# Norms applied by ScalarE, bulk transfers issued at other places in the batch loop, and the routing steps of the last batch in another order

## The reference

```python
mod = (silu(c) @ wmod).reshape(8, 6, 1, 256)            # sa, ca, ga, sb, cb, gb; ga, gb kept away from 0
h = layernorm(x) * (1 + ca) + sa
x = x + ga * attention(h)                               # 32 heads of 8, window of 8 to each side, then proj
h = layernorm(x) * (1 + cb) + sb
x = x + gb * moe(h)                                     # shared MLP (width 352) + top 2 of 16 experts (width 176)
```

## Time and profile before

| | |
|---|---|
| three runs | 449.8, 444.47 and 447.63 us; median 447.63 us |
| the profiled execution | 445.15 us, its span 443.3 us |
| busy share | PE 88%, DVE 61%, POOL 28%, ACT 27% |
| mean granted TensorE clock | 0.935 of full speed |
| batch loop | about 24 to 220 us |
| expert tiles | about 275 to 401 us |

### The profile page before, as it was taken

One profiled execution on the slowest core, in us unless ns is written; L12 is line 12 of the kernel. 1 busy time (PEld: TensorE's weight loads), 2 busy tenths in 40 slices (PEclk: granted clock), 3 DMA queues, 4 the chain that ended last, 5 costly groups with the idle time before them and its releaser, 6 DMA issues.

```text
span 443.3 us, 11573 instructions
## 1 busy us (share of the span) xinstructions
PE 388.4 (88%) x4740; PEld 285.9 (65%) x4740; DVE 269.0 (61%) x515; ACT 120.5 (27%) x261; POOL 124.1 (28%) x131
## 2 busy tenths in 40 slices
PE   7889799795999999966869595999999999999963
PEld 4568588674878888855434374677777777764452
DVE  2678699674899999998864964222222222211566
ACT  1132032220323223201232440233333334331520
POOL 6201031030303030201576670043343343341000
PEclk9999899796999999999968976899999999999968
DMA  8164819978181817160122422133333332103823
GB/s 293 47 137 143 207 50 188 311 168 195 50 205 51 204 50 181 49 176 7 38 103 98 162 90 81 47 109 96 104 106 95 104 105 59 49 2 91 289 72 119
DMA packets 53066, 52.44 MB, mean 118 GB/s; under 512 B 22148, under 2 KB 48045, under 8 KB 52406
## 3 DMA queue, kind: packets, MB, share of 16 engines
q1 hardware_dynamic: 40784, 28.68, 25.0%
q0 software_dynamic: 4528, 12.40, 9.1%
q10 hardware_dynamic: 7702, 10.62, 6.9%
HBM read 28.75 MB, written 20.79 MB: 112 GB/s over the span
## 4 chain that ended last, share of the span: by engine, by line
PE 67%; DVE 15%; issue 11%; DMA 2%; POOL 2%; ACT 1%; ACTq 0%; SPq 0%; DVEq 0%; POOLq 0%
PE bank L1371 14%; PE bank L1386 9%; PE bank L1261 7%; PE bank L1215 5%; PE bank L1150 5%; PE bank L1188 5%; PE bank L1324 4%; PE bank L1197 3%; PE bank L1168 3%; PE bank L1355 2%; PE bank L1379 2%; DMA first_region<-wmod 2%; DVE region L741 2%; PE bank L1230 2%; PE bank L1208 2%
## 5 line engine op out<-in xcount | busy, mean ns | idle before, releaser
L502 POOL DMA_INDIRECT yrows<-second_region,sloti x47 | 46.2, 984 | 91.5 <-ACT second_region L644 91.2
L1023 DVE COPY second_region<-bank 128x256 f32<-128x256 f32 x47 | 20.0, 425 | 84.8 <-PE bank L1355 84.8
L1371 PE MATMUL bank<-region,second_region 128*128 x188 | 66.5, 479 | 0.2 <-DVE second_region L1023 0.2
L1386 PE MATMUL bank<-w,second_region 88*128 x188 | 48.5, 380 | 0.6 <-ACT second_region L639 0.6
L1261 PE MATMUL bank<-xT_region,sw 128*128 128x512 f32 (+1 forms) x96 | 45.2, 626 | 0.0
L449 POOL TENSOR_TENSOR rstd2s<-ve,cft 128x2 f32<-128x2 f32 x8 | 5.7, 708 | 135.8 <-DVE ve L788 135.7
L1371 PEld LDWEIGHTS bank<-region,second_region 128*128 128x128 f32 x188 | 33.1, 196 | 13.5 <-issue 3.9
L1188 PE MATMUL bank<-region,second_region 64*32 64x128 f32 x1024 | 33.1, 276 | 8.2 <-issue 8.2
L467 POOL DMA_INDIRECT hslots<-hx,posi x32 | 35.5, 1110 | 16.3 <-issue 9.0
L1188 PEld LDWEIGHTS bank<-region,second_region 64*32 64x32 f32 x1024 | 28.0, 109 | 16.0 <-issue 16.0
L1324 PE MATMUL bank<-sw,second_region 128*128 128x256 f32 (+1 forms) x96 | 27.3, 446 | 10.2 <-DVE second_region L986 5.9
(11 more groups left out here) (159 smaller groups left out, 594.5 us busy)
## 6 DMA issues: line engine op xcount, KB each, us to landing
second_region<-hslots SPq DMA_DIRECT2D x47, 128.0 KB, 2.0
hslots<-zeros ACTq DMA_DIRECT2D x5, 1024.0 KB, 6.3
region<-vd SPq DMA_DIRECT2D x32, 128.0 KB, 5.3
region<-yrows SPq DMA_DIRECT2D x16, 256.0 KB, 6.0
modb<-moddram SPq DMA_DIRECT2D x8, 384.0 KB, 4.7
w<-w2T POOLq DMA_DIRECT2D x4, 704.0 KB, 9.3
xs<-x SPq DMA_DIRECT2D x8, 256.0 KB, 6.7
vd<-second_region SPq DMA_DIRECT2D x8, 256.0 KB, 2.2
```

The costliest lines, as they stand in the source:

```text
L502: gp.indirect_dma_start(yrows, bass.IndirectOffsetOnAxis(ap=sloti[:, s:s + 1], axis=0), yo[:, s % RING, :], None, bounds_check=TOPK * T - ...
L1023: dve.tensor_copy(rT[:, s % 2].rearrange("p c t -> p (c t)"), RTP).then_inc(rT_s, 1)
L1371: last = pe.matmul(UP(s), rT[:, s % 2, c, :], w13[:, c, bass.ds(experts[s], 1), :], start=c == 0, stop=c == C - 1)
L1386: last = pe.matmul(YP(s), hT2[0:IH, s % 2, k, :], w2[:, k, bass.ds(experts[s], 1), :], start=k == 0, stop=k == 1)
```

## The change

Four things are changed together. Line numbers of the new kernel differ from the old one's.

1. Both norms are applied by ScalarE as `x * rstd + off` with `off = -mean * rstd`, but for the first norm of batch 0. VectorE adds the negated mean (`less1`, `less2`), GpSimd a product of two columns (`off1`, `off2`). `ln1_apply(1)` stands on ScalarE between `scaled_h(0)` and `keep_q(0)`; in the loop both stand behind `keep_v`; `ln2_apply(7)` stands ahead of `silu_g(0)`.
2. The zeroing of `hslots` is issued in four parts (11 or 12 tiles of 128 KB each) in iterations 0, 4, 5 and 6, right behind `keep_q`. The first part of the experts' weights follows the first `exponent` of iteration 1.
3. `load_shared` and `load_second` wait for `keep_q(it+1)`. `load_x(b+3)` stands ahead of `modulation(b+1)` and `values_in(b+1)`.
4. In the last batch `count(0)` stands behind `turn_p(7, 0)`, `ranked(0)` and `new_tiles(0)` behind `over_sum(7, 0)`, and `placed(0)` behind `over_sum(7, 1)`.

```diff
-ZEROED = 6
+ZEROED = (0, 4, 5, 6)
@@ sync, batch loop
                     values_out(b + 1)
+                if b + 3 < B:
+                    load_x(b + 3)
+                if b + 1 < B:
                     modulation(b + 1)
                     values_in(b + 1)
-                if b + 3 < B:
-                    load_x(b + 3)
@@ gpsimd
             def rstd1(b):
                 wait(gp, ln_ve, b + 1)
-                gp.tensor_tensor(rstd[:, :], ve[:, :], nhalf, ALU.pow).then_inc(ln_rs, 1)
+                wait(gp, ln_xn, b)
+                pw = gp.tensor_tensor(rstd[:, :], ve[:, :], nhalf, ALU.pow)
...
+                pw.then_inc(ln_pw, 1)
+                gp.wait_ge(ln_pw, b)
+                gp.tensor_tensor(off1[:, :], less1[:, :], rstd[:, :], ALU.mult).then_inc(ln_rs, 1)
...
             def main(it, first, after):
+                if it in (1, 2, 3):
+
+                    gp.wait_ge(q_s, it + 2)
                 if it == 1:
                     load_shared()
@@ scalar
+            def ln1_apply(b):
+                wait(act, ln_rs, b + 1)
+                wait(act, hT_p, b)
+                for u in range(U):
+                    last = act.activation(xn[:, u], xs[:, U * b + u, :], ACT.Identity,
+                                          scale=rstd[:, u:u + 1], bias=off1[:, u:u + 1])
+                last.then_inc(ln_xn, 1)
...
+            def zero(k):
+                if k == 0:
+                    act.wait_ge(pads, 7)
+                a, z = k * NS // len(ZEROED), (k + 1) * NS // len(ZEROED)
+                act.dma_start(hslots_t[:, a:z], zeros[:, :].unsqueeze(1).to_broadcast([P, z - a, D])).then_inc(row_z, 16)
+
             def main(it, first, after):
                 if after:
                     scaled_h(it + 1)
                     keep_q(it + 1)
+                if it in ZEROED:
+                    zero(ZEROED.index(it))
                 exponent(it, 0)
+                if it == 1:
+                    act.wait_ge(mod_p, 3)
+                    act.dma_start(staged[:, :], w13T[:, 0:STAGE]).then_inc(ld_ew, 16)
...
                     keep_v(it + 1)
                 if not first:
+                    ln2_apply(it - 1)
+                if after > 1:
+                    ln1_apply(it + 2)
+                if not first:
                     turned_h(it - 1)
...
             scaled_h(0)
+            ln1_apply(1)
             keep_q(0)
...
+            ln2_apply(B - 1)
             silu_g(0)
@@ vector
+                dve.tensor_scalar(less1[:, :], mv[:, :, 0], -1.0, None, ALU.mult)
...
             def main(it, first, after):
-                if after == 0:
-                    ranked(0)
...
-                elif after == 0:
-                    new_tiles(0)
                 over_sum(it, 0)
+                if after == 0:
+                    ranked(0)
+                    new_tiles(0)
...
-                if not first:
-                    ln2_apply(it - 1)
                 residual(it, 0)
-                if after > 1:
-                    ln1_apply(it + 2)
-                elif after == 1:
+                if after == 1:
                     pick(1, 0)
                     chosen(0)
-                else:
+                over_sum(it, 1)
+                if after == 0:
                     placed(0)
-                over_sum(it, 1)
@@ tensor
                 if after:
                     turn_x(it + 1)
-                else:
-                    count(0)
                 scores(it, 1)
                 if after:
                     make_q(it + 1)
                 turn_p(it, 0)
+                if not after:
+                    count(0)
```

More of the change, by code:

```diff
@@ L713, in _ @@
             ln1_stats(0)
-            ln1_apply(0)
+            dve.wait_ge(ln_rs, 1)
+            for u in range(U):
+                last = dve.tensor_scalar(xn[:, u], xs[:, u, :], mv[:, u, 0:1], rstd[:, u:u + 1], ALU.subtract, ALU.mult)
+            last.then_inc(ln_xn, 1)
             dve.wait_ge(modT_p, 1)
@@ L734, in _ @@
             ln1_stats(1)
-            ln1_apply(1)
             def by_window(it, u):
@@ L787, in ln2_stats @@
                 wait(dve, l2_mv, it + 1)
+                dve.tensor_scalar(less2[:, :], mv2[:, :, 0], -1.0, None, ALU.mult)
                 dve.tensor_scalar(ve2[:, :], mv2[:, :, 1], EPS, None, ALU.add).then_inc(l2_ve, 1)
[L790 to L796 removed]
             links = [0]
```

49 lines of the change are left out of this document (23 added, 26 removed).

## The result

| | before | after |
|---|---|---|
| median of 12 runs each, side by side | 445.18 us (440.1 to 451.8) | 447.09 us (443.3 to 451.6) |
| ratio | | 1.0081, 95% interval 1.0041 to 1.0121 |
| the profiled execution | 445.15 us, span 443.3 | 445.70 us, span 443.9 |
| busy: PE, DVE, ACT, POOL | 88, 61, 27, 28% | 87, 57, 31, 29% |

Executions over 1.5% slower than the fastest of their kernel are left out of this ratio and of every later one (7 of 12 for "transfers only"), and both profiles of the kernel before, that of "norms only" and that of the old order are of such executions.

What follows compares the result with a forecast made beforehand. TensorE, busy 88%, was taken as the bound, with 17.6 us of loop excess at stake. Terms 4.0 + 0.3 - 0.3 - 4.5 + 0.4 = -0.1 us against 445.15; forecast set at 446.0 us, own range 441 to 450, with rivals 434.5 to 454.

Steps and rivals of the forecast that it cites:

- 1, setup: Ahead of the loop: `ln1_apply(1)` delays `keep_q(0)` to 22.5 us, +4.0 us uncovered, plus 0.3 for the clock.
- 2, norms: In the loop: VectorE loses two norm applications per batch, TensorE wins only its waits for VectorE, -0.3 us.
- 3, transfers: In the loop: moved bulk transfers leave 13.1 us of excess instead of 17.6, -4.5 us.
- 4, last batch: End of the loop: `over_sum(7, 0)` ends 3.1 us earlier, but `turn_h(7)` comes +0.4 us (bounds -0.5 and +1.2).
- forecast excess of 13.1 us: Batch loop's time over its floors after the change: 0.9 + 5.5 + 5.0 + 1.7 us, instead of 17.6.
- Iterations 2 and 3: Behind `keep_q`, `w2T` makes a block 3.9 us late or in time; half taken, 0.6 for clock: 2.5 us each.
- rival 1: Placement works: refill slips in ahead of the bulk in iterations 1, 2 and 3, excess 3 to 7 us; chance 0.30.
- Iteration 0: Shared weights' packets leave; a block waits for `values_out`, `load_x(3)` and `modb`, and 0.9 us of excess remain.
- floor of 20.04 us: Iteration 0's least period: TensorE's 21.4 us less 1.36, since `turn_h` and `gate` are missing there.
- Iteration 1: Experts' and shared weights hold a block, gap in `times_v(1, 0)` or `make_v(2)`: 4.2 plus 1.3 for clock, 5.5 us.
- Iterations 4 and 5: Iterations 4 to 6: a zeroing part drains 1 us ahead of the next wanted block, so nothing is lost.
- rival 2: Iteration 1 takes it back: its block behind a 2.7 MB burst is served last, excess 22 us, 454 us; chance 0.20.

Runs made afterwards that it cites:

- transfers only: Kernel before with only the bulk transfers moved to the change's new places (parts 2 and 3 of its list); ratio to the kernel before 1.0014.
- norms only: Kernel before with only the norms on ScalarE, the first norm of batch 1 behind `keep_v(0)`; ratio to the kernel before 0.9926.
- old order: Changed kernel with `count`, `ranked`, `new_tiles` and `placed` of the last batch in the order of before; ratio to the kernel before 1.0092.
- old transfers: Changed kernel with all bulk transfers and `load_x` issued where the kernel before issues them; ratio to the kernel before 1.0139.
- norms and order: Kernel before with the norms on ScalarE (batch 1's first norm behind `keep_v(0)`) and the last batch in the changed order; ratio to the kernel before 1.0030.
- `w2T` in pieces: Changed kernel with only GpSimd's bulk (shared and second weights, 4.0 MB) cut into 11 pieces over iterations 0 to 5; ratio to the kernel before 1.0046.
- setup repaired: Changed kernel with the first norm of batch 1 applied behind `keep_v(0)` instead of ahead of `keep_q(0)`; ratio to the kernel before 1.0040.
- spread version: Changed kernel with batch 1's first norm behind `keep_v(0)` and the 11.4 MB of bulk cut into 39 pieces; 432.88 us, ratio to the kernel before 0.9825.
- bulk late: Changed kernel with every bulk transfer (11.4 MB) issued only in iteration 7; one execution, only its loop to be read, 129.94 us.

## Why the prediction was wrong, point by point

No single pair of these runs parts the four terms cleanly. A weighted fit of four additive parts to the eight comparisons (the change, three versions with a part undone, two parts alone and two pairs) gives them, times 442 us and with 95% bounds:

| part | forecast | fitted |
|---|---|---|
| 1, setup | +4.3 us | +3.7 +/- 1.7 |
| 2, norms | -0.3 | -1.7 +/- 1.7 |
| 3, transfers | -4.5 | +0.6 +/- 1.4 |
| 4, last batch | +0.4 | +2.4 +/- 1.7 |

The fitted sum is +5.1, the change alone measured +3.6 (1.8 to 5.4). That the parts add is assumed; the change lies 1.7 standard errors below the fit, the norms alone 1.4 below it, the version with the old order 1.4 above and that with the old transfers (1.0139) 1.1 above, for which I have no cause. With any one comparison left out, the transfers' part stays between -0.3 and +1.1 us. The others move more: the setup's between +2.5 and +5.4, the norms' between -3.1 and +0.1, the order's between +1.2 and +4.1. So the firm results are that the transfers gained nothing near 4.5 us and that the setup costs.

The last two rows of the forecast are also not cut as the fit cuts them: the +0.4 holds what the norms do at the end, which the fit counts with the norms. Together they compare well: forecast +0.1, fitted +0.7 +/- 1.3, and norms and order alone measured +1.3 (-0.4 to +3.0).

**Part 3 is the step that failed.** It was put at -4.5 us; the fit has +0.6, and the transfers alone have 1.0014, which leaves the forecast outside; only the step from the change to its version with the old transfers (-2.6 +/- 3.6 for the new places) would still allow it. The forecast excess of 13.1 us came out as 16.2 in the trace. The mechanism stood: blocks late behind bursts, shown by the kernel without them. The sizes did not:
- *Iterations 2 and 3*, "in time if it slips in ahead of the bulk. I take the half": it did not slip in. q0's first packet came 1.3 us behind the start of its issue in both iterations (84.5 to 85.8 and 112.0 to 113.3 us), where the kernel before has 2.7 and rival 1 counted on 3.4; by the count of 127 that is over 1 us ahead of the requests, at 87.1 and some 115 us. 27.54 and 24.68 us are 6.1 and 3.3 over the floor, where 2.5 each and a part of the 1.7 were forecast. The two gaps of iteration 2 make 3.85 us of the 6.1, and the granted clock is 0.81 from 92 to 110 us. `w2T` in pieces takes the two iterations to 21.22 and 22.37 us, so it is this burst.
- *Iteration 0*: the block gap of 0.9 us was forecast well (0.77), but my floor of 20.04 us was not one. PE waits 1.50 us for VectorE's residual (L816) there in ten of the sixteen traces; in the other six a block comes 2.1 us or more late just ahead of it and hides part or all of this wait. The period without bulk is 22.12 us. Of the 4.7 us of excess that I put at stake, only 2.6 could be won.
- *Iteration 1*: 25.41 us, 4.0 over the floor instead of 5.5, with the gap in `turn_p(1, 1)` (L1227, 66.47 us), between the two places named, and its packet at 64.0 to 64.5 us, ahead of the 66 to 69 that were forecast with the setup's 4 us.
- *Iterations 4 and 5*: as forecast, within 0.8 us. Iteration 4, with its zeroing part, takes 22.18 us against 21.37 before.

The four traces with the new places (the change, setup repaired, old tail, transfers only) have loops of 143.3 to 146.3 us, the six with the old ones 143.6 to 149.1. So rival 1 (placement works) fell, and rival 2 too: the bursts hold other blocks for about as long. A place that is quiet for `spread_q` isn't quiet for the instruction stream, whose packets come every 3.6 to 7.4 us in the spread version (61 to 121 us).

**Part 1** was right in mechanism and place. `keep_q(0)` came at 21.98 instead of 22.5, because GpSimd's product of two columns takes 0.20 us (0.27 the first time), not 0.5. The first scores came 3.5 us later. The clock's share, 0.3, is a matter of the execution: from `keep_q(0)` to `keep_q(1)` two of seven traces with the delay take 13.97 and 13.99 us, five 12.36, with 12.31 before. The fit has +3.7 for it, the repair alone gives 0.4% (1.0081 to 1.0040), with intervals that overlap.

**Part 2** is open in size. -0.3 lies within the fit's bounds (-3.4 to 0.0), but not within those of the norms alone (0.9926 is -3.3, from -5.5 to -1.0). In the traces quiet periods fall from 21.37 to 21.40 us to 21.22 to 21.24, some 0.16 per iteration; in seven iterations that would be 1.1 us, an estimate, against the 0.3 forecast for a few of them. "TensorE can win only its waits for VectorE" does not hold once the bursts are cut into pieces, where the kernel with the norms on ScalarE has the loop shorter by 4.2 us. ScalarE's new place holds nothing: its periods without bulk are at the floor.

**Part 4** held by the trace, and in part by luck. Against `keep_q(7)` `turn_h(7)` came 1.9 us later, but 1.7 of it lies ahead of `turn_h(6)` (39.13 us behind `keep_q(7)` against 37.47), a stretch that takes 37.5 and 40.5 us in the two profiles of the kernel before, so it shows nothing. From `turn_h(6)` to `turn_h(7)` it is +0.2, where +0.4 was forecast, and the steps are those of the prediction: `placed(0)` starts 0.8 us earlier against `turn_h(6)` (0.9 forecast), the first scatter 0.35 earlier (positions: 0.3), and from there to `turn_h(7)` it takes 11.13 us against 10.56 (+0.75 forecast). What the prediction didn't see is that its sum hides two effects. From `turn_h(6)` to `turn_h(7)` seven traces with the new order take 14.07 to 14.20 us (14.45 with the bulk in that very iteration); with the old order and the norms on ScalarE three of four take 13.36 or 13.37 (the fourth 13.88), and with the norms on VectorE 13.86 to 13.98. The new order costs 0.7, for `placed(0)` stands behind `over_sum(7, 1)` and the six scatters begin 0.7 later; the norms give 0.5 back. `over_sum(7, 0)` came 2.7 us earlier against `turn_h(6)`, near the 3.1 forecast, and as forecast nothing that followed kept it. The fit's +2.4 leaves it open whether the order costs more than the trace's 0.7.

So the sum of -0.1 us missed the measured +3.6 by 3.7, and the only part clear of the noise is the transfers', wrong by some 5. That the absolute time of 446.0 us came within 1.1 of the median is luck: the forecast was put between one execution and a median of three, and the slowdown filled the difference.

## What to carry to other kernels

In this loop of many small matmuls a bulk load cost what its bursts made the instruction stream wait, at the old places as at the new ones. Cutting all of it into pieces of some 0.3 MB and spreading them helped (0.9825); looking for a quiet place, or cutting only one queue's share, didn't. Floors for such a sum come from a run without the suspected cost, not from another iteration less what is missing in it. And two profiles of one program lay 3.7 us apart in one stretch by its clock, so a difference of that size is none until a second profile has it. Last, a forecast of several parts is tested only if each part is also run alone: the sum can come near by parts that offset each other.

## What was not expected of the hardware

- A packet of 16 KB of the instruction queue came some 5 us (9 us in the kernel before) after its block was due to be asked for, while GpSimd's software queue moved 1.4 MB. When it was asked for is an estimate from the count of 127 matmuls. With all transfers in pieces of 0.26 to 0.39 MB the gaps are 2.4 us or less; the bursts cost the loop 13.3 us (143.26 against 129.94 with the bulk late).
- A product of two 128x2 operands on GpSimd takes 0.20 us (0.27 the first time), where the power of the same shape takes 0.69.
- `spread_q`'s eight small transfers take SP 7.4 to 8.3 us to issue beside a zeroing part of 1.5 MB, 5.0 to 6.4 elsewhere.
